# A two-layer deformable-sampling kernel: more store buffers, an earlier hand-over between GpSimd and VectorE, a search summed on TensorE, and shared column blending

## The reference

```python
center = einsum('nchw,oc->nohw', feature, w_center)            # 2 channels
step   = relu(einsum('nchw,oc->nohw', feature, w_step))        # 2 channels
prob   = sigmoid(einsum('nchw,oc->nohw', feature, w_prob))     # 1 channel
offset = transpose(center * step, (0, 2, 3, 1))
th = minimum(round(gh + offset[..., 0]), h - 1)
tw = minimum(round(gw + offset[..., 1]), w - 1)
tgt = mod(int32(th * w + tw), h * w)
sample = grid_flat.at[tgt].set(grid_flat)       # the last source that hits a target wins
gx, gy = 2 * sample[..., 0] / (h-1) - 1, 2 * sample[..., 1] / (w-1) - 1
sampled = grid_sample_bilinear(feature, stack((gx, gy)))
proped = sampled * prob + feature * (1 - prob)
return feature * prob + proped * (1 - prob)
```

## Time and profile before

| what | value |
|---|---|
| median of three runs | 9847.34 us (9839.02 to 9898.68) |
| the profiled execution | 9910.58 us |
| its span | 9909.0 us |
| TensorE busy | 6574.7 us (66%), granted clock 0.786 |
| VectorE busy | 5644.5 us (57%) |
| ScalarE busy | 3752.4 us (38%) |
| GpSimd busy | 4705.3 us (47%) |

### The profile page before, as it was taken

One profiled execution on the slowest core, in us unless ns is written; L12 is line 12 of the kernel. 1 busy time (PEld: TensorE's weight loads), 2 busy tenths in 40 slices (PEclk: granted clock), 3 DMA queues, 4 the chain that ended last, 5 costly groups with the idle time before them and its releaser, 6 DMA issues. The chain is left out here.

```text
span 9909.0 us, 89353 instructions
## 1 busy us (share of the span) xinstructions
PE 6574.7 (66%) x24132; PEld 2834.2 (29%) x24132; DVE 5644.5 (57%) x11270; ACT 3752.4 (38%) x7426; POOL 4705.3 (47%) x8499
## 2 busy tenths in 40 slices
PE   5666455556623677766777578467777674787888
PEld 2222122222211333332333223223333231333333
DVE  2221444336832432226899887328999994466666
ACT  3444333332211333332333023235555263654555
POOL 2333774414433023334577143247887353566665
PEclk7888678777866888886788888776777886888888
DMA  3555444655442455555555146466554264666666
GB/s 141 181 194 205 138 158 161 161 187 176 140 91 92 169 203 196 209 197 174 186 184 205 49 152 221 140 195 179 156 159 141 89 187 112 187 209 206 220 205 201
DMA packets 489217, 1673.51 MB, mean 169 GB/s; under 512 B 119580, under 2 KB 140347, under 8 KB 421396
## 3 DMA queue, kind: packets, MB, share of 16 engines
q1 hardware_dynamic: 214092, 827.29, 27.1%
q10 hardware_dynamic: 210152, 764.05, 20.3%
q0 software_dynamic: 64480, 76.57, 4.4%
HBM read 949.99 MB, written 727.71 MB: 169 GB/s over the span
## 5 line engine op out<-in xcount | busy, mean ns | idle before, releaser
L974 POOL TENSOR_TENSOR arena<-arena 128x32 f32<-128x32 f32 (+8 forms) x3197 | 970.4, 344 | 3445.6 <-PE ps L1161 3442.5
L1161 PE MATMUL ps<-arena,w_conv 128*10 128x400 f32 x3200 | 1572.4, 603 | 1172.3 <-ACT arena L1220 923.1
L1130 PE MATMUL ps<-arena,minus 128*128 128x400 f32 x3200 | 1817.3, 655 | 632.2 <-DVE arena L1026 512.8
L1024 DVE TENSOR_TENSOR ps<-ps,arena 128x400 f32<-128x400 f32 x1600 | 926.4, 579 | 2168.5 <-PE ps L1138 1239.9
L1286 ACT ACTIVATE arena<-ps 128x400 f32<-128x400 f32 x1600 | 800.2, 500 | 2592.7 <-PE ps L1124 755.1
L1220 ACT ACTIVATE arena<-ps 10x400 f32<-10x400 f32 x1600 | 776.4, 492 | 2058.5 <-PE ps L1161 1064.7
L1174 PE MATMUL ps<-ident,arena 128*128 128x128 f32 x5000 | 923.0, 334 | 871.7 <-issue 471.7
L1104 POOL DMA_INDIRECT arena<-table,gidx x800 | 1201.6, 1502 | 602.8 <-PE ps L1147 337.2
L983 POOL TENSOR_TENSOR arena<-arena 128x32 f32<-128x32 f32 (+8 forms) x3197 | 1142.1, 403 | 10.9
L1236 ACT ACTIVATE arena<-ps 128x512 f32<-128x512 f32 (+1 forms) x1400 | 733.3, 550 | 1015.7 <-PE ps L1174 745.1
L1138 PEld LDWEIGHTS ps<-ident,arena 100*128 100x128 f32 x6400 | 825.5, 163 | 880.8 <-issue 741.5
(11 more groups left out here) (205 smaller groups left out, 5844.5 us busy)
## 6 DMA issues: line engine op xcount, KB each, us to landing
arena<-x SPq DMA_DIRECT2D x200, 1600.0 KB, 12.2
arena<-table SPq DMA_DIRECT2D x400, 800.0 KB
table<-arena ACTq DMA_DIRECT2D x400, 512.0 KB
y<-arena ACTq DMA_DIRECT2D x100, 1600.0 KB, 13.8
arena<-y SPq DMA_DIRECT2D x100, 1600.0 KB
out<-arena ACTq DMA_DIRECT2D x100, 1600.0 KB
table<-arena ACTq DMA_DIRECT2D x200, 576.0 KB
conv<-arena ACTq DMA_DIRECT2D x800, 31.2 KB
```

The costliest lines, as they stand in the source:

```text
L974: last = E.tensor_tensor(tmp[:, :, at:at + size], cols[:, :, y + to:end + to:step], cols[:, :, y:end:step], ALU.subtract)
L1024: V.tensor_tensor(d, d, g, ALU.mult).then_inc(s_mix, 1)
L1130: nc.tensor.matmul(ps[:, 4 + r % 2, 0:W], minus[:, :], tile(t)[:, r * W:(r + 1) * W], start=True, stop=False)
L1161: nc.tensor.matmul(ps[0:10, 7 - count % CB, 0:size], w_conv[lt][:, :], tile(t)[:, at:at + size], start=True, stop=True).then_inc(s_conv, 1)
```

## The change

1. Store buffers. `c_out` has six buffers in place of two; they lie at partitions 0, 64 and 96 over the memory of the gate rows. `t_out` has four buffers in sweeps that do not mix (S0, S1), two in the others as before. The semaphores of loads and stores are now made once for all sweeps, with counts carried on.

```diff
-        c_out = [part(2 * W, 10) for _ in range(2)]
+        c_out = [again(a, 2 * W, 10, F32, p) for p in (0, 64, 96) for a in gates_at]
+        used[0] += 4 * W
...
+        t_out += [again(rows_at[0] + BROWS * NFIX + a * T_WORDS, T_WORDS) for a in range(2)]
...
+            TR, CR = 2 if mixing else 4, len(c_out)
...
-                        if c % 2 == 0 and nth >= 2:
-                            act.wait_ge(s_cst[nth % 2], nth // 2 * 16)
+                        if c % 2 == 0 and nth >= CR:
+                            act.wait_ge(s_cst[nth % CR], nth // CR * 16)
...
-                        if g == a and nth >= 2:
-                            act.wait_ge(s_tst[nth % 2], nth // 2 * 16)
+                        if g == a and nth >= TR:
+                            act.wait_ge(s_tst[nth % TR], (t0[nth % TR] + nth // TR) * 16)
```

```diff
-                            clock[0] = (t + behind + 2) * BROWS + 2
+                            clock[0] = (t + behind + 1) * BROWS + 3
```

```diff
-                    note(V.tensor_scalar(m3(hit[i % 2]), src, float(i + 1), float(i + 1), ALU.is_equal, ALU.mult))
...
-                    note(V.tensor_tensor(near, near, hit[i % 2], ALU.max))
-                    yield
+                for a in range(BROWS // 2):
+                    for i in range(OFFSETS):
+                        c = a * OFFSETS + i
+                        j, e = divmod(i, SIDE)
+                        if c >= 2 * HELD:
+                            dve.wait_ge(s_joined, j0 + c - 2 * HELD + 1)
+                        src = halo[:, j + RMAX - R + 2 * a:j + RMAX - R + 2 * a + 2, RMAX - R + e:RMAX - R + e + W]
+                        V.tensor_scalar(found[c % (2 * HELD)], src, float(i + 1), 2.0 ** (3 * i // 2 - 126),
+                                        ALU.is_equal, ALU.mult).then_inc(s_found, 1)
+                        born[f"found{c}"] = clock[0]
+                        if i % HELD == HELD - 1 or i == OFFSETS - 1:
+                            yield
                     yield
+                    dve.wait_ge(s_joined, j0 + (a + 1) * OFFSETS)
+                    yield from piece(V.tensor_scalar(m3(c0m)[:, 2 * a:2 * a + 2, :].bitcast(I32), ps[0:NB, 0:2, 0:W].bitcast(I32), 23, None,
+                                                     ALU.logical_shift_right), f"joined{a}")
...
             def tensor(pe, clock):
+                for a in range(BROWS // 2):
+                    if a:
+                        yield from after(pe, clock, f"joined{a - 1}")
+                    for i in range(OFFSETS):
+                        c = a * OFFSETS + i
+                        while clock[0] <= born[f"found{c}"]:
+                            yield
+                        pe.wait_ge(s_found, j0 + c + 1)
+                        for r in range(2):
+                            last = nc.tensor.matmul(ps[0:NB, r, 0:W], ident16[0:NB, 0:NB], found[c % (2 * HELD)][:, r, :],
+                                                    start=i == 0, stop=i == OFFSETS - 1)
+                        last.then_inc(s_joined, 1)
```

```diff
                 now = (t + behind) * BROWS + 3
+                if u_idx == 2 and t % 2 == 0:
+                    return "dve"
                 return "dve" if "moved" in born and now <= born["moved"] + BROWS * spell else "pool"
```

More of the change, by code:

```diff
@@ L276, in build @@
         lsrc, ltmp, lpos = (again(near_at + a * BROWS * SLOTS, BROWS * SLOTS, NB) for a in range(3))
+        found = [again(hit_at + a * W, 2 * W, NB, BF16).rearrange("p (r w) -> p r w", w=W) for a in range(2 * HELD)]
         hot = [[again(hit_at + (4 * i + j) * (W // 2), W, 128, F16) for j in range(4)] for i in range(2)]
@@ L294, in build @@
         s_gath = [sem(f"s_gath{k}") for k in range(DEPTH // GROUP)]
-        s_tst = [sem(f"s_t_st{k}") for k in range(2)]
-        s_cst = [sem(f"s_c_st{k}") for k in range(2)]
+        s_cst = [sem(f"s_c_st{k}") for k in range(len(c_out))]
         s_lst = sem("s_late_st")
@@ L374, in build @@
         s_gatest = sem("s_gatest")
+        s_found = sem("s_found")
+        s_joined = sem("s_joined")
         steps = {"v": 0}
+        s_fld = [sem(f"s_f_ld{a}") for a in range(4)]
+        s_rld = [sem(f"s_rows_ld{a}") for a in range(3)]
+        s_gld = [sem(f"s_gate_ld{a}") for a in range(3)]
+        s_yst = [sem(f"s_y_st{a}") for a in range(4)]
+        s_tst = [sem(f"s_t_st{a}") for a in range(4)]
+        counts = {"f": [0] * 4, "rows": [0] * 3, "y": [0] * 4, "t": [0] * 4}
         def indices(u):
@@ L397, in indices @@
             mark, born = {}, {}
+            OFFSETS = SIDE * SIDE
+            j0 = sum(SIDES[a // 2] ** 2 * (BROWS // 2) for a in range(u))
             STEPS = 2 * 2 + 15 + 16 * 2 + 1 + 4
@@ L495, in vector @@
                 yield from piece(V.memset(far, 0.0))
-                yield from piece(V.memset(near, 0.0))
-                yield from blanks(2)
+                yield from blanks(5)
                 dve.wait_ge(s_halo, (u + 1) * 16 * 6)
[L500 to L505, removed]
-                    note(V.tensor_scalar(m3(hit[i % 2]), src, float(i + 1), float(i + 1), ALU.is_equal, ALU.mult))
@@ L519, in vector @@
+                yield from piece(V.tensor_scalar(c0m, c0m.bitcast(I32), 2.0 / 3.0, 0.45, ALU.mult, ALU.add))
+                yield from piece(V.tensor_scalar(c0m, c0m, MAGIC, None, ALU.subtract))
+                yield from piece(V.tensor_scalar(near, c0m, MAGIC, None, ALU.add))
                 cnt, cmax = small[:, 12, 0:2], small[:, 12, 2:3]
@@ L640, in vector @@
                     yield from piece(V.scalar_tensor_tensor(c0m, c1m, 1.0, c0m, ALU.add, ALU.mult), "src")
[L641 removed]
+                    yield from blanks(2 * BLANKS)
                 else:
@@ L904, in sweep @@
             WB = 1 if mixing else 2
-            s_fld = [sem(f"s_f_ld{k}_{a}") for a in range(FR)]
-            s_rld = [sem(f"s_rows_ld{k}_{a}") for a in range(RR)] if mixing else None
-            s_gld = [sem(f"s_gate_ld{k}_{a}") for a in range(RR)] if mixing else None
-            s_yst = [sem(f"s_y_st{k}_{a}") for a in range(FR)] if mixing else None
+            TR, CR = 2 if mixing else 4, len(c_out)
+            f0, r0, y0, t0 = (list(counts[name]) for name in ("f", "rows", "y", "t"))
+            for t in range(TILES):
+                counts["f"][t % FR] += 1
+                counts["y"][t % FR] += int(mixing)
+            for n in range(2 * TILES):
+                counts["rows"][n % RR] += int(mixing)
+            for n in range(TILES * len(PIECES)):
+                counts["t"][n % TR] += int(tabling)
             if u_idx is not None:
```

48 lines of the change are left out of this document (21 added, 27 removed).

## The result

The changed kernel takes 8807.37 us (median of four runs, 8789.49 to 8828.19), against 9850.69 us for the kernel before on the same chip (four runs, 9839.02 to 9898.68): a ratio of 0.8933, 95% interval 0.8896 to 0.8971. The prediction was 8960 us, from 8700 to 9290. The profiled execution took 8820.32 us, with a span of 8818.5.

The account below looks back on a forecast made before the run. No resource was taken as full; sweeps wait on each other's hand-overs. S0 -260, S1 -165, S2 -454, S3 -38, S4 +26, S5 0 sum to -891 from 9910.6: 9020, or 8960 us as median, range 8700 to 9290.

Parts of the forecast that it names:

- No resource is full; the sweeps wait on hand-overs.: Whole kernel: no engine or DMA is full; in S0 TensorE, the busiest, is at 609 of 950 us.
- Store buffers, S0: S0: of 275 us of ScalarE's waits for conv and table stores, 260 go; a tile would take 13.5 us.
- Store buffers, S1: S1: 200 us of store waits go, less 35 us for a later "moved": gain 165, bounds 80 and 270.
- Store buffers, S2: S2: of 305.6 us of conv store waits 235 go, since `t_out` keeps two buffers there.
- The hand-over: S2 and S3: VectorE's waits for a GpSimd blend, 219.4 and 69.0 us, go: 288, bounds 200 and 300.
- The near search: S3 and S4: the search becomes TensorE's; 4.8 and 4.5 us a slot, costing +86 and +26 us.
- Blends in S3: S3: 25 blends of 6.7 us on VectorE; room in the search, half paid in seven tiles outside: +25 us.
- (a): Store waits: transfers take the wait's place and half of the store gains comes back; 9330 us; chance 0.12.
- (b): Near search: the sums run at 1.2 GHz half of the time, +330 us; 9290 us; chance 0.12.
- (c): Near search: TensorE never pauses, a sum every 0.17 us, 196 us less; 8770 us; chance 0.13.
- (d): Near search: engines go in lockstep, a slot takes 4.2 us more and the kernel is slower; 10290 us; chance 0.03.
- (e): S2 and S3: the new hand-over gives nothing, its 288 us come back elsewhere; 9250 us; chance 0.05.

Follow-up runs that it names:

- e1: The changed kernel with two conv buffers and two table buffers again, as before: 9503.85 us, ratio 0.9924 to the kernel before.
- e2: The changed kernel with GpSimd's old hand-over clock: 8874.54 us, ratio 0.9265 to the kernel before.
- e6: The changed kernel with old hand-over, old near search and S3's blends all on GpSimd, so only the buffers are left: 9044.47 us, ratio 0.9183.
- e11: The changed kernel with S3's blends on GpSimd, new search only in S3 and S4, S1's generator pace 0.7 for 0.42: 8260.39 us, ratio 0.8621.
- e7: The changed kernel with old near search and S3's blends all on GpSimd, keeping buffers and new hand-over: 8653.81 us, ratio 0.8790.
- e3: The changed kernel with S3's column blends all on GpSimd, as before: 8388.06 us, ratio 0.8751.
- e8: The changed kernel with S3's blends on GpSimd, new search only in S3 and S4, S1's generator pace 0.55 for 0.42: 8623.29 us, ratio 0.8747.
- e5: The changed kernel itself, run again unaltered on chip B: 8812.90 us, ratio 0.8942 to the kernel before.
- e4: The changed kernel with the old near search, one compare and one maximum on VectorE, no sums on TensorE: 8474.69 us, ratio 0.8850.

## Why the prediction was right, and where it was not

**No resource is full; the sweeps wait on hand-overs.** Right. S0 to S2 lose 924 us, at 258, 183 and 211 GB/s where it was 180, 162 and 163, and e1, e2 and e6 put it down to the buffers and the hand-over.

**Store buffers, S0.** I took 260 of 275 us; S0 lost 287. A tile takes 667/50 = 13.3 us, against the 13.5 forecast. The excess goes with the clock, 0.92 in place of 0.83.

**Store buffers, S1.** The sum (165) was near 138, but by two errors against each other. The charge of 35 us for the later "moved" was too small: TensorE stands 92 us at the end, and e11 takes 89 us out of S1 by an earlier "moved" together with the old search. The gain ahead of that end must then have been larger than the 200 that I took, some 230 (138 + 92); no run takes it apart.

**Store buffers, S2.** I took 235 us. e6 gives 340 with the stall still in. The step that failed is taking the convolutions' idle time (185.2 us in 800) as all that the wait costs; TensorE's clock rose too, from 0.78 to 0.85. `t_out` did not bind: its waits in the whole execution are 72.8 us, though two are left in mixing sweeps.

**The hand-over.** I took 219 + 69 = 288, bounds 200 and 300. e7 against e6 gives 164 + 58 = 222 in S2 and S3: the waits' lengths were an upper bound. My guess is that part of what stood ran later in spare time; no run shows it. And it gives 158 in S1 that I had not seen at all: I had moved "moved" in S1 by 6.5 tiles on paper, and charged a longer end, but never asked whose tile it would then fall into under the old hand-over. In the changed kernel the wait doesn't exist, so the sum was not hurt.

**The near search.** Three sizes were off. Four compares take 1.20 us (L521 above), not 1.4. The eight sums take 1.49 us, not 1.92, as two slots of S4 in TensorE's timeline show, from the first sum to the next gate matmul:

```profile
6301.29 1.56 PE L829 MATMUL ps<-arena,ident 100*100 100x400 bf16 x8
6302.77 0.34 PE L1158 MATMUL ps<-arena,halves 6*128 6x400 bf16 x1
...
6305.08 1.56 PE L829 MATMUL ps<-arena,ident 100*100 100x400 bf16 x8
6306.57 0.34 PE L1158 MATMUL ps<-arena,halves 6*128 6x400 bf16 x1
```

A sum every 1.48/8 = 0.185 us, against 0.21 and 0.27 in the earlier trace rows, the row that I took. The f16 pair there waited for VectorE each time, and I carried that wait over. And the clock: I held both searches at a row of 2.6 and 2.9 us, times of before that hold pauses. The slot of S4 above is 3.80 us, where I had 4.5. Over S4's search a tile takes 31.9 us, so 3.99 a slot, and 4.35 before. In S3 I had 4.8: in tiles 18 to 26 one of GpSimd's takes 33.8/8 = 4.22 a slot, one of VectorE's 40.7/8 = 5.09. From the first to the last compare it is 862.7 us over 177 rows, 4.87, and 789.8 over 178, 4.44, in e3. So 4.8 was near only with the blends' price in it, which I had counted apart. The forecast had set "under 4.3" as a sign that it was wrong in the search, and in S4 it was. The search's term, +86 and +26, is in truth +43 in S3 (e8 against e7) and -38 (B) to some -84 (A) in S4. "I count them at nothing" of S1 and S2 was short by some 30 us in S1 and 1 to 38 in S2 (e8 against e5 on B, e4 against e3 on A).

The Trainium skill (TensorE: Matmul & The Clock Gate, section Back-to-back issue gap) gives N/2.4 + 2.5 ns for the gap of an isolated matmul at the full clock, by which 400 columns take an estimated 169 ns. The stream here shows 185, nearer to it than the row on which I relied.

**Blends in S3.** I took +25 us, bounds 0 and 168, and it is +137 to +150. The step that failed is "In the search VectorE has room for them", which priced the tiles there at nothing; they cost 73 us. It had room on the mean, and still has (1455 of 2119 us busy). It has none for a piece of 6.6 us in one slot when TensorE waits behind it, for the blend itself at the turning, or for the compare behind the blend, with only eight small buffers between. The tiles outside the search, priced at 25, cost 77.

So S3 came out near its forecast (-46 against -38) by terms that cancel, which is luck. In the order buffers, hand-over, search, blends I had -80, -69, +86 and +25; the steps from the kernel before to e6, e7, e8 and e5 are -156, -58, +43 and +137, which is -34 with e5's S3 of 2147.

**S5.** Nothing was predicted, -49 was measured, with the same instructions. Between chips the same sweep varies by 200 us, and the profiled execution of before was 60 us above its median, so I count none of it to the change. Some of S4's -71 may be of that kind.

**The signs.** As forecast, `conv` waits are under 50 us (12.6) and VectorE waits nowhere for a blend of GpSimd. In the searches TensorE is nearly full (778 of 863 us in S3, 666 of 699 in S4). VectorE's busy time fell by 394 us (5644.5 to 5250.5), not by some 600. My own terms give only about 440: 344 x 1.82 less for the maxima, 344 x 0.23 more for the compares, 16 x 6.7 more for the blends.

**The rivals.** (a) fell: the wait for table stores went down too (72.8 us, from 151.7 in all), at more GB/s. (b) fell: from the first to the last compare the clock is 0.92 in S3 and 0.99 in S4 (0.82 and 0.74 before), not 0.80 and below. (c) had the right direction and half the right reason: 0.185 us a sum, where it said 0.17; its 8770 us were nearer than my 8960. (d) fell: a compare is a slot ahead, except behind some of the blends, where its mechanism acts for one slot of the tile. (e) fell: e2 and e7 against e6 both show the hand-over's gain. Of the 199 us between the sums (1090 and 891), S4 gives 97, S5 49, S2 45, S0 27, S3 8 and S1 -27.

## What to carry to other kernels

A store wait that more buffers hide can be worth more than its length, since the pauses also cost clock on TensorE: 287 us of sweep for 275 of waiting in S0, and, with the buffers alone (e6), 340 for 306 of `conv` waits in S2 and 156 for 139 in S3. It can be worth less where something else ends the sweep: in S1 138 for 303, where "moved" also came later. When an engine that others wait for gets more work, look for the longest single piece on it, not for its mean load; here 25 pieces of 6.6 us on an engine with room cost 137 to 150 us of the sweep. And when a change shifts an event in time, read again every decision that is taken by that event: the third stall of the hand-over was in a sweep where the profile of before showed none.

## What the runs showed of the hardware

- At the two pauses shown, of 3.21 us (e1, at 4929) and 3.63 us (changed, at 4390), TensorE's granted clock was 1.00 before, and 0.50 and 0.53 in stretches of 4 and 6 us behind (1.00 is 2.4 GHz, 0.50 is 1.2); what follows takes 1.8 times as long (0.94 to 1.70 us, 0.84 to 1.50) for the next 5 us.
- A stream of eight 400-column bf16 matmuls, each with its weight load and a semaphore at every second one, goes at 0.185 us each, at a granted clock of 1.00 (changed, S4, at 6301).
- The same instructions take different times on different chips, most of all in the last sweep. S5 of e11 on C has the same instructions as S5 of the changed kernel (the last of its windows, in the section on the result), and VectorE is as busy (841.82 us against 838.43):

```profile
7206.00:8267.00 1061.00, 964.37 (x4400) 427.83 (x4400) 841.82 (x1600) 655.40 (x1198) 804.32 (x790) 0.96 0.80 256
```

But it takes 1061 us in place of 1272, at a clock of 0.96 against 0.87 and with 256 GB/s against 214. Which of the two leads, the transfers or TensorE's clock, is open; I did not try it. A ratio to the kernel before on the same chip is needed, and even that shifts by some thousandths when a part of the time that the change doesn't touch is longer on one chip.
